# Transposing a tile's rows right behind its own last sums, and running the last pair of tiles one by one

## The reference, cut to what matters

```
msgs  = x[src]                                   # 100000 x 512
neigh = segment_sum(msgs, dst, 6250)             # 6250 x 512
rst   = (1 + eps) * x + neigh
h     = relu(rst @ W1 + b1)                      # 512 -> 1024
h     = h @ W2 + b2                              # 1024 -> 512
out   = layernorm(x + (h + x))                   # per row, 512 features
```

## Time and profile before

| what | value |
|---|---|
| time, median of 3 runs | 1096.75 us (1094.89 to 1099.66) |
| time of the profiled execution | 1097.57 us |
| its span, first to last instruction | 1095.6 us |
| busy share of the span | PE 88%, PEld 55%, POOL 72%, DVE 33%, ACT 23% |
| mean granted TensorE clock | 0.957 of full speed |

### The profile page before, as it was taken

How to read it: one execution, slowest core, us unless ns; L and a number is a source line. 1 busy time by engine, 2 the same in 40 slices (tenths; PEclk the granted TensorE clock), 3 DMA queues, 4 the chain that set the end, 5 groups by cost and what they waited for, 6 DMA issues and landing times.

```text
span 1095.6 us, 17920 instructions
## 1 busy us (share of the span) xinstructions
PE 960.4 (88%) x6338; PEld 604.8 (55%) x6338; DVE 364.1 (33%) x930; ACT 253.6 (23%) x512; POOL 789.6 (72%) x819
## 2 busy tenths in 40 slices
PE   1458898999989899889989889899889899889887
PEld 1115565556646556556647546556546556546556
DVE  3523232342332332332333333332333332332332
ACT  1103122222222222222212212212212212212212
POOL 5677777777777777777777777777777777777720
PEclk9869999998999999999999999899999899999899
DMA  6876877877877877877877877877877777787730
GB/s 183 266 235 202 248 222 233 246 229 229 247 238 213 246 234 210 248 235 220 244 241 209 248 242 211 245 239 215 242 242 205 239 238 212 239 248 207 239 98 19
DMA packets 86622, 243.91 MB, mean 223 GB/s; under 512 B 18178, under 2 KB 20953, under 8 KB 86593
## 3 DMA queue, kind: packets, MB, share of 16 engines
q0 software_dynamic: 64544, 210.95, 64.8%
q1 hardware_dynamic: 22049, 32.56, 9.2%
HBM read 229.83 MB, written 13.62 MB: 222 GB/s over the span
## 4 chain that ended last, share of the span: by engine, by line
POOL 59%; issue 21%; PE 12%; DMA 5%; DVE 1%; POOLq 0%; SPq 0%; ACT 0%; DVEq 0%; ACTq 0%
POOL raw L435 59%; PE hp L1060 6%; DMA raw<-in_x_dram,idx 3%; PE acc L1095 3%; PE y L1076 2%; DMA raw<-in_src_dram 1%; DMA raw<-in_dst_dram,rowidx 1%; POOL pair_shared L467 0%; POOL shared L476 0%; POOLq L265 0%; PE tables L993 0%; DVE moments L880 0%; DVE late L876 0%; POOLq L267 0%; POOL raw L446 0%
## 5 line engine op out<-in xcount | busy, mean ns | idle before, releaser
L435 POOL DMA_INDIRECT raw<-in_x_dram,idx x800 | 777.9, 972 | 249.9 <-issue 247.0
L1095 PE MATMUL acc<-raw,onehot 128*32 128x512 f32 x2200 | 324.5, 646 | 90.1 <-DMA raw<-in_x_dram,idx 88.2
L1060 PE MATMUL hp<-rstT_hi,w_hi 128*128 128x250 f32 x800 | 232.7, 291 | 4.4 <-DVE rstT_lo L856 4.2
L1060 PE MATMUL hp<-rstT_lo,w_hi 128*128 128x250 f32 x800 | 228.7, 286 | 0.0
L1060 PE MATMUL hp<-rstT_hi,w_lo 128*128 128x250 f32 x800 | 228.4, 285 | 0.0
L861 DVE TENSOR_TENSOR hT_lo<-late,hT_hi 128x500 fp32r<-128x500 f32 x100 | 68.1, 681 | 334.3 <-ACT hT_hi L561 334.3
L556 ACT ACTIVATE late<-hp,b1c 128x250 f32<-128x250 f32 x200 | 83.0, 467 | 399.2 <-PE hp L1060 399.2
L1060 PEld LDWEIGHTS hp<-rstT_hi,w_hi 128*128 128x128 f32 x800 | 155.3, 194 | 25.6 <-ACT late L556 16.8
L1060 PEld LDWEIGHTS hp<-rstT_lo,w_hi 128*128 128x128 f32 x800 | 155.5, 194 | 20.1 <-issue 20.1
L1076 PE MATMUL y<-w_hi,hT_hi 128*125 128x512 f32 x400 | 162.5, 406 | 0.0
L1076 PE MATMUL y<-w_hi,hT_lo 128*125 128x512 f32 x400 | 160.4, 401 | 0.0
(11 more groups left out here) (103 smaller groups left out, 453.7 us busy)
## 6 DMA issues: line engine op xcount, KB each, us to landing
raw<-in_x_dram,idx POOLq DMA_INDIRECT x800, 3.7
xt<-in_x_dram SPq DMA_DIRECT2D x50, 224.0 KB
out_dram<-late SPq DMA_DIRECT2D x50, 224.0 KB
late<-in_L_gnn_W_dram SPq DMA_DIRECT2D x7, 512.0 KB, 6.4
xt<-in_x_dram SPq DMA_DIRECT2D x50, 26.0 KB
out_dram<-late SPq DMA_DIRECT2D x50, 26.0 KB
win<-pairs SPq DMA_DIRECT2D x52, 16.0 KB, 3.5
pairs<-raw SPq DMA_DIRECT2D x1, 781.2 KB
```

The costliest lines, as they stand in the source:

```text
L435: pool.indirect_dma_start(out=raw[:, i, k, :], out_offset=None, in_=table[:, :], in_offset=bass.IndirectOffsetOnAxis(ap=idx[:, slot, k:k + ...
L1060: mm = pe.matmul(hp[jp % 2][:, jj, :], w1[a][:, c, j * P:(j + 1) * P], rstT[b][:, half, c, :], start=(c == 0 and term == 0), stop=(c == TC ...
L1095: return pe.matmul(acc[i][q * QN:(q + 1) * QN, :], hot, rows, start=((q, k) == of_q[0]), stop=((q, k) == of_q[-1]))
```

## The change

A tile is now transposed in the last step of its own sums: at steps 3 and 7, behind the sums and some products of the layers (5 of layer 1 at step 3, what is left of layer 2 at step 7), PE issues `rst_T` of that tile and then goes on. The shares of layer 1 move one step earlier, so that layer 1 of a group begins at step 0 of the next one, and those of layer 2 begin at step 3. ACT's and DVE's lists are put in the matching order: `rst_hi` and `rst_lo` stand right behind `make_rst`, the third `relu_pair` and `h_lo` ahead of it, and the one-hots of the next tile behind it.

The last pair is cut into two single tiles. `layer1_solo(i)` makes the 96 products of layer 1 for tile 48 (i=0) or 49 (i=1) alone, each with 126 columns instead of 250; `layer2_solo(f)` the 24 of layer 2 of one tile. In the last group, step 6 finishes layer 2 of the pair before and takes 40 products of tile 48's layer 1; step 7 takes 12 more, then transposes tile 49, then takes the other 44. After the group come 8 products of tile 48's layer 2, all 96 of tile 49's layer 1, the other 16 of tile 48's layer 2 and the 24 of tile 49's. `relu_solo` and `h_lo_solo` do ReLU, copy and remainder for one tile, on half the columns; there are eight of each in place of four.

```
-L1_SHARE = (0, 24, 34, 34, 4, 0, 0, 0)
-L2_SHARE = (0, 0, 0, 0, 6, 12, 17, 13)
+L1_SHARE = (24, 26, 34, 12, 0, 0, 0, 0)
+L2_SHARE = (0, 0, 0, 8, 12, 12, 12, 4)
+UNTIL_TURN = 5
+SOLO_BEFORE = 40
+SOLO_UNTIL_TURN = 12
+SOLO_L2_BEFORE = 8
...
@@ ACT, after the last group
+            relu_solo(0, 0)
             root(TILES - 3, 1)
             normalise(TILES - 3, 1)
-            rst_hi(TILES - 1, 1, last % 2, last - 1, False)
-            for jp in range(PAIRS):
-                relu_pair(last, jp, False)
+            relu_solo(0, 1)
+            rst_hi(TILES - 1, 0, (last + 1) % 2, last, False)
+            for i, jp in ((0, 2), (0, 3), (1, 0), (1, 1), (1, 2), (1, 3)):
+                relu_solo(i, jp)
...
+            def relu_solo(i, jp):
+                k = PAIRS * (GROUPS - 1 + i) + jp
+                cols = slice(i * TN, (i + 1) * TN)
+                act.wait_ge(s_mm1, 2 * k + 2)
+                act.wait_ge(s_hlo, k - 1)
+                for jj in range(2):
+                    act.activation(hfull[:, jp % 2, jj, cols], hp[jp % 2][:, jj, 0:TN], ACT.Relu,
+                                   bias=b1c[:, 2 * jp + jj:2 * jp + jj + 1]).then_inc(s_relu, 1)
+                act.wait_ge(s_relu, 2 * k + 2)
+                act.wait_ge(s_y, TILES - 2)
+                act.activation(hT[0][:, 2 * jp:2 * jp + 2, cols], hfull[:, jp % 2, :, cols],
+                               ACT.Copy).then_inc(s_hhi, 1)
...
@@ DVE, after the last group
-            make_rst(TILES - 1, 1, (TILES - 1) % 4, (TILES - 1) // 4, False)
             residuals(TILES - 3, 1, (TILES - 3) % 4, 32 * (last - 1))
             take_moments(TILES - 3, 1)
+            h_lo_solo(0, 0)
             scale_shift(TILES - 3, 1)
-            rst_lo(TILES - 1, 1, last % 2)
+            h_lo_solo(0, 1)
+            make_rst(TILES - 1, 1, (TILES - 1) % 4, (TILES - 1) // 4, False)
+            rst_lo(TILES - 1, 0, (last + 1) % 2)
             double_x(TILES - 1, (TILES - 1) % 4)
-            for jp in range(PAIRS):
-                h_lo(last, jp)
+            for i, jp in ((0, 2), (0, 3), (1, 0), (1, 1), (1, 2), (1, 3)):
+                h_lo_solo(i, jp)
...
@@ PE, a group
-                    if b == 0:
-                        rst_T(T - 1, 1 - i, False)
-                    elif b == 1:
+                    if b == 1:
                         window_T(T + 2)
-                    take(one, L1_SHARE[p])
+                    n = 0
+                    if b == NB - 1:
+                        n = min(UNTIL_TURN, L1_SHARE[p])
+                        take(one, n)
+                        if i == 1:
+                            take(two, L2_PRODUCTS)
+                        if not (solo and i == 1):
+                            rst_T(T, i, False)
+                    take(one, L1_SHARE[p] - n)
                     take(two, L2_SHARE[p])
+                    if solo and p == STEPS - 2:
+                        take(two, L2_PRODUCTS)
+                        take(solo, SOLO_BEFORE)
+                    if solo and p == STEPS - 1:
+                        take(solo, SOLO_UNTIL_TURN)
+                        rst_T(T, i, False)
+                        take(solo, L1_PRODUCTS)
...
+                    mm = pe.matmul(hp[jp % 2][:, jj, 0:TN + 1], w1[a][:, c, j * P:(j + 1) * P],
+                                   rstT[b][:, (GROUPS - 1 + i) % 2, c, 0:TN + 1],
+                                   start=(c == 0 and term == 0), stop=(c == TC - 1 and term == 2))
...
@@ PE, after the last group
-            rst_T(TILES - 1, 1, False)
-            take(layer1(last, last % 2, False), L1_PRODUCTS)
-            take(layer2(last, False), L2_PRODUCTS)
+            left, right = layer2_solo(0), layer2_solo(1)
+            take(left, SOLO_L2_BEFORE)
+            take(layer1_solo(1), L1_PRODUCTS)
+            take(left, L2_PRODUCTS)
+            take(right, L2_PRODUCTS)
```

More of the change, by code:

```diff
@@ L589, in group @@
                     cut_weights(3)
[L590 to L593, removed]
                 if not (static and g < 1):
@@ L598, in group @@
                         cut_weights(q)
+                if not (static and g < 2):
+                    root(T0 - 3, 1)
+                    normalise(T0 - 3, 1)
+                window_f32(T0 + 2, (res + 2) % 4, lap + (res + 2) // 4)
                 if not (static and g < 1):
@@ L601, in group @@
                     relu_pair(g - 1, 1, static and g == 1)
+                    relu_pair(g - 1, 2, static and g == 1)
                 window_f32(T0 + 3, (res + 3) % 4, lap + (res + 3) // 4)
-                if not (static and g < 1):
-                    relu_pair(g - 1, 2, static and g == 1)
-                    relu_pair(g - 1, 3, static and g == 1)
                 if static and g == 0:
@@ L610, in group @@
                 if not (static and g < 1):
+                    relu_pair(g - 1, 3, static and g == 1)
                     root(T0 - 2, 0)
                     normalise(T0 - 2, 0)
+            def relu_solo(i, jp):
[10 more added lines that the diff above has]
+                               ACT.Copy).then_inc(s_hhi, 1)
             window_f32(0, 0, 0, True)
@@ L917, in group @@
                     make_rst(T0 - 1, 1, (res + 3) % 4, lap + (res - 1) // 4, static and g < 2)
+                    rst_lo(T0 - 1, 1, 1 - half)
+                    if static and g == 1:
+                        for q in (6, 7):
+                            cut_weights(q)
                 one_hots(T0 + 1, 1, (res + 1) % 4, static and g < 1)
@@ L928, in group @@
                     scale_shift(T0 - 3, 1)
[L929 to L933, removed]
                 window_tables(T0 + 2, (res + 2) % 4)
@@ L938, in group @@
                     h_lo(g - 1, 1)
+                    h_lo(g - 1, 2)
                 if static and g == 0:
@@ L945, in group @@
                         one_hots_shared(t, t)
+                    one_hots(T0 + 2, 0, (res + 2) % 4, False)
+                    one_hots_shared(T0 + 2, (res + 2) % 4)
+                    make_rst(T0, 0, res, lap, True)
+                    rst_lo(T0, 0, half)
                 else:
                     make_rst(T0, 0, res, lap, False)
[L948 to L953, removed]
+                    rst_lo(T0, 0, half)
                     h_lo(g - 1, 3)
-                rst_lo(T0, 0, half)
-                if not (static and g == 0):
+                    one_hots(T0 + 2, 0, (res + 2) % 4, False)
+                    one_hots_shared(T0 + 2, (res + 2) % 4)
                     window_tables(T0 + 3, (res + 3) % 4)
@@ L962, in group, with h_lo_solo @@
                     scale_shift(T0 - 2, 0)
+            def h_lo_solo(i, jp):
+                dve.wait_ge(s_hhi, PAIRS * (GROUPS - 1 + i) + jp + 1)
+                cols = slice(i * TN, (i + 1) * TN)
+                dve.tensor_tensor(hT[1][:, 2 * jp:2 * jp + 2, cols], hfull[:, jp % 2, :, cols],
+                                  hT[0][:, 2 * jp:2 * jp + 2, cols].bitcast(F32), ALU.subtract).then_inc(s_hlo, 1)
             dve.wait_ge(s_small, 32)
@@ L1138, in first_group, with group @@
                 rst_T(0, 0, True)
-            def group(g, res, lap, halves):
+                rst_T(1, 1, False)
+            def group(g, res, lap, halves, solo=None):
                 T0 = 2 * g
@@ new lines, in group, with layer1_solo @@
+                    take(one, L1_SHARE[p] - n)
+                    take(two, L2_SHARE[p])
+                    if solo and p == STEPS - 2:
[5 more added lines that the diff above has]
+                        take(solo, L1_PRODUCTS)
+            def layer1_solo(i):
+                for n in range(L1_PRODUCTS):
+                    j, c, term = n // (TC * 3), n // 3 % TC, n % 3
+                    jp, jj = j // 2, j % 2
+                    if n == 0:
+                        pe.wait_ge(s_rlo, TILES - 1 + i)
+                    if c == 0 and term == 0 and jj == 0:
+                        pe.wait_ge(s_relu, 2 * (PAIRS * (GROUPS - 1 + i) + jp - 1))
+                    a, b = ((0, 0), (0, 1), (1, 0))[term]
+                    mm = pe.matmul(hp[jp % 2][:, jj, 0:TN + 1], w1[a][:, c, j * P:(j + 1) * P],
+                                   rstT[b][:, (GROUPS - 1 + i) % 2, c, 0:TN + 1],
+                                   start=(c == 0 and term == 0), stop=(c == TC - 1 and term == 2))
+                    if c == TC - 1 and term == 2:
+                        mm.then_inc(s_mm1, 1)
+                    yield
@@ new lines, in layer2_solo @@
+            def layer2_solo(f):
+                for n in range(L2_PRODUCTS // 2):
+                    j, term = n // 3, n % 3
+                    if n == 0:
+                        pe.wait_ge(s_z, TILES - 3 + f)
+                    if j % 2 == 0 and term == 0:
+                        pe.wait_ge(s_hlo, PAIRS * (GROUPS - 1 + f) + j // 2 + 1)
+                    a, b = ((0, 0), (0, 1), (1, 0))[term]
+                    mm = pe.matmul(y[f][0:TN, :], hT[a][:, j, f * TN:(f + 1) * TN], w2[b][:, j, :],
```

(14 more changed lines are left out.)

## The result

| | before | after |
|---|---|---|
| median (four runs each) | 1095.82 us (1094.62 to 1099.66) | 1107.18 us (1105.88 to 1108.85) |
| ratio, 95% interval | | 1.010 (1.0077 to 1.0123) |
| profiled execution, its span | 1097.57, 1095.6 | 1108.15, 1106.2 |
| end of POOL's last gather | 1049.6 | 1052.9 |
| from there to the span's end ("tail") | 46.0 | 53.3 |

The changed kernel is slower by 1%, 11.4 us between the medians. 1098 was forecast, with a range of 1088 to 1104: the prediction was wrong in size and in kind, no change having been forecast.

A forecast was written before the change was run, and what follows sets the result against it. POOL bounds until 1049.6, then PE's 46.0 us tail. Loop 0; 4.6 gap, 2.3 half clock, 1.7 earlier start go; 11.2 of loads, partly hidden, and 2.1 wait come: span 1096.8 (+1.2), forecast 1098, range 1088 to 1104.

The forecast's parts named there:

- the new wait: Last group, before tile 49's transposes: PE stands 2.1 us for make_rst, which waits on DVE behind the second h_lo_solo.
- The rival that gave it the clock as well: Tail: clock falls to 0.50 at the transposes' wait and stays through 44 + 96 products, +13.6 us, 1111.6; chance 0.09.
- the load path is full: Argument against a clock fall in the tail: during layer 1 weight loading is busy 7.90 of 7.90 us.
- The pitch: Tail, layer 1 products with 126 columns: weight loads set their spacing, 0.1162 us each, as with 250 columns.
- Columns do not set it: Denies a rival for the tail: columns pace products at 0.0586 us, total 1088.7; 0.17 together with the 81 ns case.
- 81 ns for a stream of load and product: Rival for the tail's single products: 6.6 us less, total 1091.4; chance 0.17 together with column pacing.
- The rest of the tail: After POOL's last gather, wait and pitch apart: transposes from 1062.6, layer 2 done at 1090.6, span's end at 1096.8.
- the end: After the last layer 2 product: residual, normalisation and store take 6.2 us, as before.
- The main loop, costed at 0 +- 4: Up to POOL's last gather: POOL sets the time, new PE waits are covered, so no change, with 4 us scatter.
- that phase: Main loop: shifted DVE timing against POOL's gathers could move it over 5 us; chances 0.06 shorter, 0.07 longer.
- the expected gain: Tail: the 4.6 us gap, 2.3 us of half clock and some 1.7 us from step 6 beginning earlier go.
- The gap: Before the last pair's layer 1: PE idle until 1064.41 because rst_hi stands behind tile 47's normalisation on ACT; 4.6 us.

The follow-up runs named there:

- experiment 3: The changed kernel with 32 columns in place of 126 in the single-tile products, so the last two tiles are not fully computed: 1117.57 us in one run.
- experiment 4: The changed kernel with the last pair in one piece again and rst_hi, rst_lo of tile 49 moved earlier: 1090.00 us, ratio 0.9957 to the kernel before.
- Experiments 4 and 7: Second of the two: kernel before, rst_hi and rst_lo of tile 49 moved earlier, tile 49 transposed at step 7 behind four layer 2 products: 1087.42 us, 0.9929.
- experiment 5: The kernel before with only rst_hi of tile 49 ahead of tile 47's normalisation on ACT and rst_lo right behind make_rst on DVE: 1090.58 us, 0.9964.
- experiment 1: The changed kernel with make_rst of tile 49 moved ahead of the second h_lo_solo on DVE: 1097.49 us, ratio 1.0027 to the kernel before.
- experiment 2: The changed kernel with 250 columns in place of 126 in the single-tile products, the wait left: 1104.19 us, ratio 1.0079 to the kernel before.

## Why the prediction was wrong

**The step that failed is the price of the new wait.** It was forecast in its place and nearly in its length (2.1 us, measured 1.82), and priced at that length alone. The rival that gave it the clock as well had 0.09 and was set aside on two grounds. The first was that sums behind a gap of 2.56 us ran at the full clock. That was one row, and a lucky one. The same trace has a gap of 2.57 us behind which they did not; the timeline of PE before, and the windows behind this gap and behind the one of 2.56:

```profile
328.35 1.31 PE L1095 MATMUL acc<-raw,onehot 128*32 128x512 f32 x8 [2.57 <-DMA raw<-in_x_dram,idx]
```
```profile
328.40:332.40 4.00, 4.00 (x21) 1.52 (x22) 0.67 (x3) 0.00 (x0) 3.01 (x4) 0.58 0.86 277
654.60:658.60 4.00, 4.00 (x34) 2.54 (x35) 0.94 (x3) 0.00 (x0) 3.15 (x3) 1.00 0.87 277
```

Between 130 and 1040 us that trace has six gaps of PE of 1.7 to 2.7 us, of which two have a fall of the clock in them or within 2 us behind them, and 13 longer ones, of which 11 have. So the row was no evidence against the rival. Three traces with 1.80 to 1.82 us here show the clock fall. The second ground was that the load path is full: it was busy in experiment 3 too, and the clock fell there with no gap at all. Price by rows of after: transposes 1.10, 44 products 9.29, 8 of layer 2 3.38, together 13.77 us, where the full clock gives 0.45 + 44 x 0.1111 + 1.86 = 7.20. That is 6.6 us. The rival's own price of 13.6 had the clock stay low through all 140 products; it came back before the last 96.

**The pitch was right.** Columns do not set it: 0.1111 us with 126, 0.1117 with 32, where columns would have given 0.0586 for 126. The load of the same 128 columns of weights fits; no run changed the load itself, so another fixed cost of a product is not ruled out. 0.1162 was taken, so the 96 products came out 0.5 us shorter than forecast. The Trainium skill, "TensorE: Matmul & The Clock Gate", section "LDWEIGHTS (loading the stationary operand)", gives a load as its columns over 1.2 GHz, an estimate of 107 ns for 128; the trace agrees within 5%. The same page of the Trainium skill, section "Back-to-back issue gap", gives 81 ns for a stream of load and product with 128 columns; the trace does not agree, and the measurement decides.

**The rest of the tail was right.** From POOL's end to the transposes 13.0 us were forecast, 13.4 measured; the last 40 products 9.32, measured 9.35; the end 6.2, measured 6.1. Forecast for the tail 47.2, measured 53.3; the difference of 6.1 is the clock (13.77 for 7.55 as forecast, 6.2) less 0.5 of pitch, plus 0.4 ahead of the transposes.

**The main loop, costed at 0 +- 4.** Between the two profiled executions POOL ends 3.3 us later: 1.9 of it lies ahead of the first gather of tile 2 (71.5 against 73.4 us), 1.4 in the loop behind that. The first is scatter: over all twelve traces this point lies between 69.8 and 73.4 with no tie to the order. For the loop, four traces of the old order give 976.7 to 978.9 us, mean 978.0; eight of the new one 977.6 to 983.0, mean 980.2. What the 768 gathers from tile 2 on take beyond 0.946 us sums to 17.8 us in the mean of the old order and 20.0 of the new, which is the whole difference. In all twelve traces gathers that began while an `h_lo` ran took longer, 1.12 to 1.19 us in the mean against 0.95 to 0.96 for the others; but what these lost sums to 12.7 us in the mean of the old order and 13.2 of the new, so that phase explains little of the difference. Experiments 4 and 7 have equal tails and different loops, and ratios of 0.9957 and 0.9929 whose intervals overlap. So some 2 to 3 us of loss in the loop are likely and not settled.

Of the 11.4 us between the medians, the tail holds 7.6 (means of two traces each, 51.95 less 44.35), the loop about 2.2 by the means above, and 1.6 are not placed.

**Where the expected gain went.** The gap was the order of the lists, as read from the earlier trace rows, and closing it alone is worth 3.4 us (0.36%, experiment 5). The change closed it too, but paid for it with 96 more weight loads (96 x 0.1111 = 10.7 us) and opened a wait of its own. Without that wait (experiment 1) the split still is 0.3% slower than before, only just clear of no change, while the pair in one piece behind the same loop (experiment 4) is 0.4% faster.

**Open.** The length of a gap does not settle whether the clock falls. In the main loops of the eight traces of the new order, 15 of 59 gaps of 1.7 to 2.0 us have a fall in them or within 2 us behind them; at the transposes of tile 49 it was three of three. What PE did before and after differs between the two places, and no run separated that from chance. The fall in experiment 3, with no gap ahead of it, stays unexplained too.

## What to carry to other kernels

A short wait on PE is priced by its length and by the clock of what follows: look at which products stand behind it, and give both prices. For the chance of the second, count all gaps of about that length in the trace: one that cost nothing says little. Cutting products in half by columns saved 5% here and not half, since columns did not pace them, and behind the wait the narrower ones ran longer at the half clock. Before work is split to fill a gap, see what ends the gap: here it was the place of one copy in ACT's list.

## What the runs showed of the hardware

- Between 130 and 1040 us, every fall of the clock in the twelve traces (92) lies in a gap of PE or within 2 us behind one. Of the 301 gaps of 0.5 to 1.5 us none has one; of those of 1.7 to 2.0 us in the new order 15 of 59; of those over 2.3 us in the old order 57 of 67.
- Behind the wait or the gap in the tail the clock stayed low for 10 to 14 us where products of 126 columns came first (after, twice), and for 3 to 5 us of products where they had 250 (experiment 2, and before, twice), PE being busy in each.
- Products of 126 columns ran 10.67 us at 1.00 (experiment 1) once the clock was there; those of 32 columns lost it without a gap (experiment 3).
- A fresh 128x128 block of float32r weights a product gives a pitch of 0.112, 0.111 and 0.117 us for 32, 126 and 250 columns at the full clock, and of 0.211 for 32 and 126 at the half clock.
